# Beta terms of two conditioned projections from PSUM row sums on VectorE, and an output offset added by two wide matmuls

## The reference

```python
# layer 0, per batch b: conditions (64x128), x (64 batches, 64 tokens, 256)
dg, db = cond @ down_gamma, cond @ down_beta          # 64 x 64
ug, ub = cond @ up_gamma,  cond @ up_beta             # 64 x 256
down = einsum(x, down_project * dg[b] + db[b])        # weight (256, 64) of batch b
up   = einsum(relu(down), up_project * ug[b] + ub[b]) # weight (64, 256) of batch b
x = x + (up + x)
# layer 1: x += x @ (U_b V) + bias_b ; layer 2: modulated projection, attention over 16 heads
#          (16 x 16 per token), second modulated projection ; then layer 3 ends in
h = silu(cat @ W1 + b1) @ W2 + b2                     # b2 is the output offset
out = x + layernorm(h) * g + be
```

## Time and profile before

| | us |
|---|---|
| runs shown | 574.38, 600.00, 602.05 (median 600.0) |
| profiled execution | 574.75 |
| its span, first to last instruction | 573.0 |
| PE busy | 463.9 (81%) |
| DVE busy | 344.4 (60%) |
| ACT busy | 290.1 (51%) |
| POOL busy | 170.0 (30%) |
| mean granted PE clock | 0.923 |

### The profile page before, as it was taken

One profiled execution on the slowest core, in us unless ns is written; L12 is line 12 of the kernel. 1 busy time (PEld: TensorE's weight loads), 2 busy tenths in 40 slices (PEclk: granted clock), 3 DMA queues, 4 the chain that ended last, 5 costly groups with the idle time before them and its releaser, 6 DMA issues.

```text
span 573.0 us, 9362 instructions
## 1 busy us (share of the span) xinstructions
PE 463.9 (81%) x3768; PEld 260.9 (46%) x3768; DVE 344.4 (60%) x641; ACT 290.1 (51%) x433; POOL 170.0 (30%) x146
## 2 busy tenths in 40 slices
PE   4297667715189999999999999999999968985682
PEld 3176334313136555545655555465546445532241
DVE  1146438581048749847965984697498466715813
ACT  0000278302685578667848874793976578301010
POOL 3003989000221512233151223224222322512301
PEclk9999788957569999999999999999999999988797
DMA  5960230004812553290446328243622723212001
GB/s 193 330 203 38 63 121 2 18 10 117 249 38 78 145 151 110 63 262 27 138 127 168 90 70 213 76 150 82 177 75 78 208 52 114 57 55 74 0 1 37
DMA packets 68736, 61.00 MB, mean 106 GB/s; under 512 B 53910, under 2 KB 55572, under 8 KB 68308
## 3 DMA queue, kind: packets, MB, share of 16 engines
q1 hardware_dynamic: 64404, 43.86, 27.8%
q0 software_dynamic: 3712, 12.59, 6.9%
q10 hardware_dynamic: 576, 3.95, 1.7%
HBM read 39.18 MB, written 21.07 MB: 105 GB/s over the span
## 4 chain that ended last, share of the span: by engine, by line
PE 61%; DVE 15%; DMA 7%; ACT 7%; SPq 5%; issue 4%; POOL 1%; POOLq 0%; DVEq 0%; ACTq 0%
PE ph L589 15%; PE pk L568 8%; PE ph L551 6%; PE ph L677 5%; ACT bd L803 3%; PE pp L551 3%; DMA k_dram<-kxb 2%; PE pp L708 2%; PE pp L691 2%; DMA kt<-k_dram 2%; DMA v<-in_V 2%; PE pp L598 2%; PE pp L649 2%; PE ph L671 2%; PE pp L723 1%
## 5 line engine op out<-in xcount | busy, mean ns | idle before, releaser
L803 ACT ACTIVATE bd<-kc,ownrow 128x512 f32<-128x512 f32 x128 | 80.6, 709 | 0.3
L816 ACT ACTIVATE bd<-vc,ownrow 128x512 f32<-128x512 f32 x128 | 80.7, 710 | 0.0
L393 POOL TENSOR_TENSOR demod<-demod,neghalf 128x32 f32<-128x32 f32 x8 | 43.2, 5452 | 46.7 <-DVE demod L972 46.7
L568 PE MATMUL pk<-bd,kc 128*32 128x128 f32 x1024 | 35.7, 298 | 22.5 <-ACT bd L803 22.5
L568 PEld LDWEIGHTS pk<-bd,kc 128*32 128x32 f32 x1024 | 30.5, 120 | 36.3 <-ACT bd L803 25.9
L551 PE MATMUL ph<-attnT,owT 128*128 128x512 f32 x64 | 34.5, 688 | 5.0 <-DVE h L1121 5.0
L559 PE MATMUL pk<-ident,osb 128*128 128x128 f32 x128 | 21.5, 293 | 17.7 <-DVE osb L1049 15.7
L431 POOL TENSOR_TENSOR attnT<-attnT,style 128x1024 f32<-128x1024 f32 x8 | 15.2, 1901 | 67.4 <-DMA attnT<-av_dram 67.4
L589 PE MATMUL ph<-tT,w 128*128 128x512 f32 x64 | 32.6, 657 | 2.1 <-DVE tT L1069 2.1
L551 PE MATMUL pp<-ys,kwT 128*128 128x512 f32 x64 | 31.6, 639 | 2.6 <-DVE ys L1180 2.6
L568 PE MATMUL pk<-bd,et 128*32 128x128 f32 x1024 | 32.1, 279 | 0.0
(11 more groups left out here) (200 smaller groups left out, 911.5 us busy)
## 6 DMA issues: line engine op xcount, KB each, us to landing
xin<-in_x SPq DMA_DIRECT2D x8, 512.0 KB, 4.6
x_dram<-x SPq DMA_DIRECT2D x8, 512.0 KB, 2.6
k_dram<-kxb SPq DMA_DIRECT2D x16, 256.0 KB, 3.4
kt<-k_dram SPq DMA_DIRECT2D x8, 512.0 KB, 4.1
v_dram<-kxb SPq DMA_DIRECT2D x8, 512.0 KB, 5.0
vt<-v_dram SPq DMA_DIRECT2D x8, 512.0 KB, 5.7
x1r<-x_dram SPq DMA_DIRECT2D x8, 512.0 KB, 3.6
av_dram<-av SPq DMA_DIRECT2D x8, 512.0 KB, 5.8
```

What stands on the lines that cost most here:

```text
L393: gp.tensor_tensor(q, q, neghalf[:, 0:4 * CB].rearrange("p (l a b) -> p l a b", l=2, a=2), ALU.pow).then_inc(gs_dem, 1)
L568: ins = mm(pk[32 * r:32 * r + 32, o:o + 128], weights(h, 4 * i + r)[:, 16 * pair:16 * pair + 32], bd[:, h, 8 * i + 2 * r + pair, :], start ...
L803: fn(bd[:, h, :, 16 * b:16 * b + 16].rearrange("p (q z) x -> p q z x", z=2), kc[:, 16 * h:16 * h + 16, :].rearrange("p q (z x) -> p q z x" ...
L816: fn(bd[:, h, :, 16 * b:16 * b + 16], vc[:, SH * h:SH * h + SH, :], ACT.Copy, scale=ownrow[:, 1, b:b + 1]).then_inc(s, 1)
```

## The change

The beta tables are now stored transposed, feature on partition and batch along the free dimension (`dbT` on partitions 64 to 127, `ubT` on all). The row sums are multiplied by them on VectorE, straight from PSUM, and added there. `w_up` gets 128 columns of ones, so the sums of act0 stand on all partitions of P0. The matmuls L659 and L708 are gone, and the last addition to x0 stands ahead of the work on the output projection in VectorE's list. The offset of y is put down by one bf16 matmul of 512 columns for two groups of 128 tokens, ahead of their fp32 matmuls. In the first step, pieces of a preparatory product (`first_factor`) follow one place earlier.

```diff
-        w_up = sb("w_up", [H0, D + H0])
-        db_rows = sb("db_rows", [128, H0])
-        ub_rows = sb("ub_rows", [128, D])
+        w_up = sb("w_up", [H0, D + 128])
+        dbT = sb("dbT", [128, B])
+        ubT = sb("ubT", [128, 2, B])
...
@@ TensorE, step @@
                     if first(a):
                         first_factor(0)
+                        first_factor(1)
...
-                if a is not None:
-                    after(pe, v_row_in, a)
-                    settled(pe)
-                    mm(P1[0:H0, :], db_rows[64:128, :], row_in, start=True, stop=True).then_inc(p_db, 1)
-                    if first(a):
-                        first_factor(1)
...
+                        if j % 2 == 0:
+                            mm(ph[:, D * j:D * j + 512], ones3[:, :], b2_parts[:, :], start=True, stop=False, skip_group_check=True)
                         for k in range(2):
-                            mm(o, hid[:, k, 128 * j:128 * j + 128], w2[:, k, :], start=(k == 0), stop=False)
-                        ins = mm(o, ones3[:, :], b2_parts[:, :], start=False, stop=True)
+                            ins = mm(o, hid[:, k, 128 * j:128 * j + 128], w2[:, k, :], start=False, stop=(j % 2 == 1 and k == 1),
+                                     skip_group_check=True)
...
-                    mm(P0[64:128, :], w_up[:, D:D + H0], act0, start=True, stop=True).then_inc(p_up, 1)
+                    mm(P0, w_up[:, D:D + 128], act0, start=True, stop=True).then_inc(p_up, 1)
                     if first(a):
                         first_factor(2)
+                        first_factor(3)
+                        demod_sums()
...
-                if a is not None:
-                    after(pe, v_row_mid, a)
-                    for o in range(2):
-                        ins = mm(P01[:, 512 * o:512 * o + 512], ub_rows[64:128, 128 * o:128 * o + 128], row_mid, start=True, stop=True)
-                    ins.then_inc(p_ub, 1)
-                    if first(a):
-                        first_factor(3)
-                        demod_sums()
@@ VectorE, step @@
-                    tt(by_batch(row_in), by_batch(P0[64:128, :]), per_batch(batch_eye[64:128, :], 64, a), ALU.mult
-                       ).then_inc(v_row_in, 1)
+                    tt(by_batch(act0), by_batch(P0[64:128, :]), per_batch(dbT[64:128, :], 64, a), ALU.mult
+                       ).then_inc(v_bt, 1)
                     after(ve_, a_act0, a - 1)
                     tt(by_batch(t1), by_batch(P0[0:H0, :]), per_batch(dg[:, :], H0, a), ALU.mult).then_inc(v_t1, 1)
...
-                    after(ve_, p_db, a)
                     after(ve_, v_t1, a)
-                    tt(t1, t1, P1[0:H0, :], ALU.add).then_inc(v_t2, 1)
+                    after(ve_, v_bt, a)
+                    tt(t1, t1, act0, ALU.add).then_inc(v_t2, 1)
...
-                    tt(by_batch(row_mid), by_batch(P0[64:128, :]), per_batch(batch_eye[64:128, :], B, a), ALU.mult
-                       ).then_inc(v_row_mid, 1)
+                    tt(by_batch2(ys[:, :, :]), by_batch(P0).unsqueeze(1).to_broadcast([128, 2, CB, S]), per_batch2(ubT[:, :, :], a),
+                       ALU.mult).then_inc(v_us, 1)
...
                     stt(x0[:, :, :], xT[:, :, :], 2.0, x0[:, :, :], ALU.mult, ALU.add).then_inc(v_x0a, 1)
                     if first(a):
                         first_factor(2)
+                    after(ve_, v_x0a, a)
+                    after(ve_, v_us, a)
+                    tt(x0[:, :, :], x0[:, :, :], ys[:, :, :], ALU.add).then_inc(v_x0, 1)
...
-                if a is not None:
-                    after(ve_, p_ub, a)
-                    after(ve_, v_x0a, a)
-                    tt(x0[:, :, :], x0[:, :, :], halves(P01), ALU.add).then_inc(v_x0, 1)
```

More of the change, by code:

```diff
@@ L54, in build @@
         ident = sb("ident", [128, 128])
-        batch_eye = sb("batch_eye", [128, B])
+        batch_eye = sb("batch_eye", [64, B])
         rowclass = sb("rowclass", [128, 1])
@@ L74, in build @@
         tables = sb("tables", [56, 3 * D + NC * D], BF16)
-        b2_parts = sb("b2_parts", [3, D], BF16)
+        b2_parts = sb("b2_parts", [3, 2 * D], BF16)
         last_gb = sb("last_gb", [128, 2, D])
@@ L86, in build @@
         xT = sb("xT", [128, 2, N])
[L87 to L90, removed]
+        down0 = sb("down0", [H0, N])
+        mid0 = sb("mid0", [H0, N])
+        t1 = down0[:, :]
+        act0 = mid0[:, :]
         x0 = sb("x0", [128, 2, N])
@@ L212, in build @@
         p_hnT = sem("p_hnT"); v_sT = sem("v_sT"); p_hs = sem("p_hs"); v_hT = sem("v_hT"); p_down = sem("p_down")
[L213 to L217, removed]
+        p_hid = sem("p_hid"); a_bk0 = sem("a_bk0"); p_s0 = sem("p_scores0"); v_hid = sem("v_hid")
+        p_y0 = sem("p_y0"); p_y = sem("p_y"); v_sub0 = sem("v_sub0"); p_tg = sem("p_tg"); a_act0 = sem("a_act0")
+        a_hnT = sem("a_hnT"); p_up = sem("p_up"); v_p0 = sem("v_p0"); a_gtm = sem("a_gtm"); p_eT0 = sem("p_eT0")
+        v_yn = sem("v_yn"); a_bk1 = sem("a_bk1"); p_s1 = sem("p_scores1"); v_up = sem("v_up"); p_x2k = sem("p_x2k")
         v_x0 = sem("v_x0"); p_u = sem("p_u"); a_et0 = sem("a_et0"); a_bv0 = sem("a_bv0"); p_av0 = sem("p_av0")
@@ L221, in build @@
         a_ex0 = sem("a_ex0"); v_sub1 = sem("v_sub1"); a_ex1 = sem("a_ex1"); v_h1a = sem("v_h1a")
-        v_bn = [sem(f"v_bn{i}") for i in range(3)]; v_t1 = sem("v_t1"); v_max0 = sem("v_max0")
-        v_sum0 = sem("v_sum0"); v_rz0 = sem("v_rz0"); v_x0a = sem("v_x0a"); v_max1 = sem("v_max1")
-        v_sum1 = sem("v_sum1"); v_rz1 = sem("v_rz1")
+        v_bn = [sem(f"v_bn{i}") for i in range(3)]; v_bt = sem("v_bt"); v_t1 = sem("v_t1"); v_max0 = sem("v_max0")
+        v_sum0 = sem("v_sum0"); v_rz0 = sem("v_rz0"); v_us = sem("v_us"); v_x0a = sem("v_x0a")
+        v_max1 = sem("v_max1"); v_sum1 = sem("v_sum1"); v_rz1 = sem("v_rz1")
         def after(eng, s, c, n=1):
@@ L269, in build @@
         layer_loads = (
-            (batch_eye[:, :], t["batch_eye"]), (w_down[:, :, 0:H0], t["down"]), (bdec, t["bdec"]),
+            (batch_eye[:, :], t["batch_eye"][0:64, :]), (w_down[:, :, 0:H0], t["down"]), (bdec, t["bdec"]),
             (w_up[:, 0:D], t["up"]), (kwT[:, :, :], t["kwT"]), (owT[:, :, :], t["owT"]), *((v1[32 * r:32 * r + K1, :], t["V"]) for r in range(4)))
@@ L304, in small_tables @@
                                      p[:, 3 * D:4 * D].unsqueeze(1).to_broadcast([n, NC, D])).then_inc(s_tab, 16)
-                    sp.dma_start(b2_parts[s:s + 1, :], b2p[:, s, :]).then_inc(s_tab, 16)
+                    sp.dma_start(b2_parts[s:s + 1, :].rearrange("p (z j) -> p z j", z=2),
+                                 b2p[:, s, :].unsqueeze(1).to_broadcast([1, 2, D])).then_inc(s_tab, 16)
                 sp.wait_ge(s_vec, 16)
@@ L370, in _ @@
             gp.memset(w_down[:, :, H0:128], 1.0).then_inc(s_const, 1)
-            gp.memset(w_up[:, D:D + H0], 1.0).then_inc(s_const, 1)
+            gp.memset(w_up[:, D:D + 128], 1.0).then_inc(s_const, 1)
             gp.memset(ones3[:, :], 1.0).then_inc(s_const, 1)
@@ L466, in _ @@
             mm(ph[0:H0, 0:64], dgam, condT, start=True, stop=True)
-            mm(ph[64:128, 64:128], condT, dbet, start=True, stop=True)
+            mm(ph[64:128, 64:128], dbet, condT, start=True, stop=True)
             for a in range(2):
@@ L473, in _ @@
                     mm(ph[:, q:q + 64], affT[:, l, 128 * a:128 * a + 128], condT, start=True, stop=True)
-            mm(ph[64:128, 576:832], condT, ubet, start=True, stop=True).then_inc(ps_par, 1)
+            for a in range(2):
+                ins = mm(ph[:, 576 + 64 * a:640 + 64 * a], ubet[:, 128 * a:128 * a + 128], condT, start=True, stop=True)
+            ins.then_inc(ps_par, 1)
             def first_factor(i):
@@ L930, in _ @@
             cp(dg[:, :], ph[0:H0, 0:64])
-            cp(db_rows[64:128, :], ph[64:128, 64:128])
+            cp(dbT[64:128, :], ph[64:128, 64:128])
             cp(ug[:, :, :], ph[:, 128:256].rearrange("p (a b) -> p a b", a=2))
@@ L936, in _ @@
                     ts(style[:, l, a, :], ph[:, q:q + 64], cols[:, 4 * l + a:4 * l + a + 1], None, ALU.add)
-            cp(ub_rows[64:128, :], ph[64:128, 576:832]).then_inc(vs_par, 1)
+            cp(ubT[:, :, :], ph[:, 576:704].rearrange("p (a b) -> p a b", a=2)).then_inc(vs_par, 1)
             ve_.wait_ge(vs_par, 1)
```

## The result

The changed kernel takes 581.06 us (median of 20 runs), the kernel before 577.17 (20 runs). Compared like with like the ratio is 1.0081, with a 95% interval of 1.0055 to 1.0108: 0.8% slower, clear of no change and inside the 2% that the forecast called "no change". Some executions of every kernel here, two of the three shown ahead of the prediction among them, lie on a second, higher level of time, which the ratios leave out and the medians in us do not: in the four profiles of such executions the same four matmul records ahead of the first key product take 3.78 us and not 1.98, that product starts at 75 to 79 us and not at 58 to 63, and the full steps behind it read like those of other executions.

A forecast was written before the change was run, and what follows sets the result against it. In full steps TensorE looked full, but VectorE's work up to x2T was only 0.25 us from limiting it. Work terms summed to -0.8 us, the clock +6.5: +5.7 on 574.75, 580 us; range 571 to 608.

The forecast's parts named there:

- no change: Whole kernel: time within 2% of before, between 563 and 586 us on the lower level; chance 0.75.
- The clock: Full steps 3 to 7: TensorE's new 3.4 us wait drops the granted clock, 1.3 us a step, +6.5 in all.
- the rival about GpSimd: Moved x0 addition, both inputs in SBUF, slowed by GpSimd: 2.16 us in eight steps, 598; chance 0.16 with other VectorE costs.
- the rival of full matmul gain: Full steps: VectorE is not the limit, each gains 2.8 us of matmul time, 557 in all; chance 0.08.
- the clock does not fall: Rival for the full steps: no loss at half rate, 574.75 - 0.8 = 574 us; chance 0.26.
- A full step with the clock up: Steps 3 to 7: x2T transposes (L723) start 0.62 us later; step 6 +1.16; together +3.6 us.
- the offset: In y on TensorE: two bf16 matmuls of 512 columns replace four slots, 0.84 - 0.52 = 0.32 us won.
- Step 6: Full step where first scores wait 0.60 us for ScalarE, so L659's 0.54 is not won: +1.16 us.
- Step 0: First step: L659 and L708 stand on the chain and nothing of VectorE replaces them: -2.9 us.
- Step 2: VectorE idle 3.31 us ahead of L1145 swallows the 1.68 of added work, so L723 starts earlier: -0.9 us.
- the drain: Steps 8 to 10, no chunk in layer 0, gain only from the offset: 3 x 0.32 = -1.0 us.
- Step 1: Chain runs through VectorE's additions to x0, which lengthen by 0.42: +0.4 us.

The follow-up runs named there:

- the filled kernel: The changed kernel plus three extra fp32 matmuls of 512 columns, read by nobody, in TensorE's wait for x2T in steps 3 to 7: 573.08 us, ratio 0.9929.

## Why the prediction was right or wrong

**The number.** The sum was +5.7 us on the profiled 574.75, 580 in all; the profiled execution rose by 6.0, and the ratio says 0.8%, some 4.7 us on 577. The step that failed is the last one, from the sum to the time of the runs. The prediction saw two levels in the runs shown, set its sum on the lower one although the shown median of 600.0 lay on the upper, and left open on which level the changed kernel would be read, with 606 for the upper. So the number that it gave stood 20 us below the time before, while the argument forecast a rise. The runs showed in its place that both kernels are read near the lower level, with medians of 577.17 before and 581.06 after; the upper one, for which the range was stretched to 608, was not where either median fell. The second fault is the same thing in the chances: 0.75 on "within 2%" holds, but the text called a rise of 1% "no change" where 20 runs of each tell 0.8% from nothing.

**The mechanism** of the full steps held. L659 gave half its length, because `hid` waits for the tanh (0.49 us bracket at L668). VectorE runs without idle time from y to x2T. TensorE waits for x2T in each full step. The clock fell behind that wait, in four steps of five. The moved addition, with two SBUF inputs, takes 1.22 to 1.23 us in all eight steps, and the addition ahead of it, also with two SBUF inputs, takes 1.22 us while GpSimd issues the output DMA, so the rival about GpSimd is refuted; the rival of full matmul gain too. The rival "the clock does not fall" forecast 574; the filled kernel, which is that case in the full steps, gives 573.08 in its profiled execution, and by its ratio 571 on 574.75.

**The terms of the sum** were less good than the sum, and that 580 came so near to the profiled 580.74 is in part luck: their errors cancel. A full step with the clock up costs +0.20 us (50.75), not +0.62: y lasts 4.49 us, not 4.68, so the offset gives 0.51 and not 0.32 (the pair of fp32 matmuls after it fills a slot of 0.97, not 1.06), and the start of the norm to x2T grew by 1.53, not 1.68. The clock costs 8.8 us over five steps, 1.75 a step, not 1.3, because two of the four falls lasted through transposes, x0 products and values together, 2.8 us each, and the other two cost 1.6 each, all beyond the 1.54 that I had set as the upper bound from one row. Full steps in all: +8.9 for a forecast of +10.1. Step 6 had no wait for ScalarE this time. Step 0 gave 3.3 for 2.9. Step 2 gave 0.4 for 0.9, and the drain 2.8 for 1.0.

Step 1 cost 3.7 for 0.4 (kx at 59.20 and 127.21, against 62.50 and 126.84), and all of it is the clock. TensorE waits for x0 there; first the kernel before, then the changed one:

```profile
97.62 0.65 PE L733 MATMUL pp<-x,u_all 128*32 128x64 f32 x32 [1.45 <-DVE x L1154]
98.09 1.93 PE L568 MATMUL pk<-bd,et 128*32 128x128 f32 x64
...
103.75 1.89 PE L536 MATMUL ph<-w,xnT 128*5 128x256 f32 x8 [2.55 <-DVE x1r L1012]
```

```profile
94.30 1.08 PE L728 MATMUL pp<-x,u_all 128*32 128x64 f32 x32 [5.20 <-DVE x L1138]
95.16 3.64 PE L570 MATMUL pk<-bd,et 128*32 128x128 f32 x64
...
102.58 3.42 PE L538 MATMUL ph<-w,xnT 128*5 128x256 f32 x8 [2.56 <-DVE x1r L1007]
```

x0 is ready 35.1 us behind kx in both, so the longer product on VectorE cost nothing. But with L708 gone, and the second scores at full rate (1.96 us, 3.12 before), TensorE waits 5.20 us there and not 1.45, and behind it the groups up to the next addition (L1176 before, L1170 now) take 2.15 us more and L538 1.53 more, at half rate. I had priced the clock only in the full steps, and left it out in the steps where it already came and went, where it cost more in one step than in any full one.

## What to carry to other kernels

A share of 99% busy on one engine does not say that its work can be taken away with profit: look at how late the next engine already is at each place where they meet; here VectorE was only 0.25 us ahead of TensorE at the place where 1.9 us of matmul went. When VectorE takes over work from TensorE, put the piece that nobody waits for behind the piece that TensorE waits for, and measure the order, since the order was worth 2.3% here (1.0081 to 0.9846, two additions on VectorE and one group on TensorE moved), while taking the matmuls away in the first order lost 0.8%. And price the clock behind a new idle stretch of TensorE as well as the stretch.

## What the hardware showed that I had not expected

Waits of 1.92 us, once per step, were enough for the granted clock to fall in all five steps of the profile (1.2 GHz behind it, period 51.09), while waits of 0.88 and 0.9 us never did (periods 49.48 and 49.60, clock 1.00). Yet one of the five waits of 3.17 us in the changed kernel left the clock up, so the length of the wait alone does not decide it. So a wait far shorter than the 3.16 us of step 1 can cost another 1.5 us behind it (51.09 against 49.60 with half of it filled), and matmuls that compute nothing of use, put into it, made two kernels faster by some 9 and 7 us. And a gain of 0.53 us in each full step, seen in two profiles, left the time where it was (0.9996), while the drain behind it, which the edit does not touch, ran 5.7 us longer at another mean clock (0.85 against 0.90).
